# A six-sublayer decoder on one core: in the feed-forward, the down product moves behind the next tile's gate and up, the sigmoids move ahead of the rounding, and the layer norm's last step moves from the vector to the scalar engine

## The chip, the core and the metric

The kernel runs on one core of one Trainium2 chip. The metric is the device time of one execution in microseconds (us), of which the median over several runs is taken. The engines meant below are TensorE (PE in the profile; PEld is its weight loads), VectorE (DVE), ScalarE (ACT), GpSimd (POOL) and the sync engine's DMA queue (SP). Each engine works through its own instructions in the order in which they were written; semaphores (`G["..."]`) join them.

## The reference, cut to what matters

The model is two decoder layers of three sublayers each on x of 4 sequences of 256 tokens and 256 features; after each sublayer the sum is layer-normed. The change touches the third sublayer, a feed-forward in which weights are rounded to -1, 0, 1 and activations to 8 bits:

```python
def _quant_act(x):
    scale = jnp.maximum(jnp.max(jnp.abs(x), axis=-1, keepdims=True), EPS) / 127.0
    return clip(round(x / scale), -128, 127) * scale      # forward value
gate = jax.nn.sigmoid(bitlinear(x, w_gate))     # 256 -> 1024
up = bitlinear(x, w_up)                         # 256 -> 1024
out = bitlinear(gate * up, w_down)              # 1024 -> 256
x = _layernorm(x + out)       # (v - mean) / sqrt(var + eps)
```

The sublayer behind it is an attention over latent keys and values. Its weights are folded on the chip first (a product of `w_qT` with `w_kd` and of `w_vd` with `w_oh` for each pair of heads), and that folding is done inside the feed-forward's loop.

## The kernel before

The 1024 tokens are eight tiles of 128 rows (`NT` = 8, t = 0 to 7), two to a sequence. The feed-forward runs as a loop over t from 0 to 8 written out by hand on four engines; nothing but the written order and the semaphores sets the order of work. For tile t:

- `f_gate_up(t)` (PE, L1883): eight bf16 products of 512 columns into banks 1 to 4 (the gate and the up in two halves c). It needs the sigmoid of the tile before for the gate's banks and the product `hh` of the tile before for the up's banks.
- `f_gate(t)` (ACT, L862): two sigmoids of 128x512, `f_sig`.
- `f_hidden(t)` (DVE, L1287): two products `hh` = gate * up (L1292), the largest of each row (L1295), four tiny steps to the row's scale (`f_hsc`, L1299) and one more (L1300).
- rounding (ACT, L880): `hr` = `hh` times the scale plus a magic number, `f_hround`.
- `f_hidden_quant(t)` (DVE, L1303): the magic number off again, `hq` in bf16, `f_hq`.
- `f_hiddenT(t)` (PE, L1974): eight bf16 transposes into bank 5; ACT copies them to `hqT` (L876).
- `f_down(t)` (PE, L1985): eight products into bank 6, `f_y`.
- `f_out(t)` (DVE, L1308): adds the residual (L1311), then the row's mean and variance (L1050, L1051), `ln_var`.
- `rstd_of(16 + t)` (POOL, L520): variance plus epsilon (L524), power -0.5 (L527), `ln_rstd`.
- `ln_end(16 + t)` (DVE, L1053): the normed row into `x_row` (L1056), `ln_done`.

Two more tasks run in the same loop. `d_fold(t)` (PE, L1992) is the folding for pair t of heads: four f32 products of 64 columns and two of 256 into bank 7, each recorded as two matmuls, which ACT copies out (`d_folded`, L837, lines L839 and L842). `d_fold(0)` waits for the transfers of `w_oh`, `w_qT` and `w_qr` (issued at L456 to L460, when the sublayer before has ended), and each later one for the copies of the one before. POOL's `rotate` (L567) works on folded weights in the first six steps, each ahead of `rstd_of` of the same step; its first one waits for the same transfers. Also in the loop are transposes of the quantized input of later sequences (`f_transpose`, copied by ACT's `f_rowsT`) and of finished sequences (`to_xT`, copied by ACT's `xT_copy`), and, in step 1, the last two tiles' input quantization (`f_round` on ACT L761, `f_quant` on DVE L1171).

The order within step t of the loop is, before the change: on PE `f_hiddenT(t-1)`, `f_down(t-1)`, `f_gate_up(t+1)`, `d_fold(t-1)`, transposes. On ACT: copy of `hqT(t-1)`, rounding of t, `f_gate(t+1)`, (step 1: two `f_round`), `d_folded(t-1)`, copies of transposes. On DVE: `f_hidden(t)`, `f_out(t-1)`, `f_hidden_quant(t)`, (step 1: two `f_quant`), `ln_end(t-1)`. After the loop PE goes on with `d_fold(7)` and `d_latent(0)`, the first product of the next sublayer, which waits for `d_folded(7)`.

Of the kernel before, what the change touches and what calls it, by code (L numbers as in the profile page):

```python
# [35 lines left out]
ACT = mybir.ActivationFunctionType  # L36
ALU = mybir.AluOpType
# [6 lines left out]
NT = B * TPB  # L44
# [87 lines left out]
def build(nc, d, xs, ys, out):  # L132
    with ExitStack() as ctx:
        def sb(name, shape, dt=F32):
            return ctx.enter_context(nc.sbuf_tensor(name, shape, dt))
# [7 lines left out]
        def sem(name):  # L143
            return ctx.enter_context(nc.semaphore(name))
# [40 lines left out]
        mhalf = sb("mhalf", [P, 1])  # L185

        x_ids = sb("x_ids", [P, NT, E + 2])
        x_row = x_ids[:, :, 0:E]
        xT = sb("xT", [P, KT, B * S])
        res = sb("res", [P, 4, E])  # L190
        stats = sb("stats", [P, 4, 6])
        mv = sb("mv", [P, 4, 2])
        nmr = sb("nmr", [P, 4])
        rstd = sb("rstd", [P, 4])
# [168 lines left out]
        G = {n: sem(n) for n in names}  # L363
# [141 lines left out]
        def _(pool):  # L505
            g = nc.gpsimd
# [10 lines left out]
            pool.dma_start(cbias[:, :], d["cbias"]).then_inc(G["ld_cbias"], 16)  # L517
            steps = [0]

            def rstd_of(n):  # L520

                s = n % 4
                pool.wait_ge(G["ln_var"], n + 1)
                g.tensor_scalar(rstd[:, s:s + 1], mv[:, s, 1:2], LN_EPS, None, ALU.add).then_inc(G["pool_step"], 1)  # L524
                steps[0] += 1
                pool.wait_ge(G["pool_step"], steps[0])
                g.tensor_tensor(rstd[:, s:s + 1], rstd[:, s:s + 1], mhalf[:, :], ALU.pow).then_inc(G["ln_rstd"], 1)  # L527


            def a_mixed_values(b):  # L530
# [52 lines left out]
            for n in range(NT):  # L583
                if n < 2:
                    rotate(w_ki[:, :, LAT:P], w_kr[:, :, :], LAT, KV1, n)
                elif n < 2 + 2 * KT:
                    k, half = divmod(n - 2, 2)
                    rotate(w_qe[:, k, :, LAT:P], w_qr[:, k, :, :], P, H1, half)
                rstd_of(2 * NT + n)

            def norm_p(p):
                for h in (2 * p, 2 * p + 1):
# [52 lines left out]
            for t in range(NT):  # L645
                n = 5 * NT + t
# [7 lines left out]
        def _(act):  # L654
            a = nc.scalar
# [140 lines left out]
            for b in range(B):  # L796
# [7 lines left out]
                for c in range(CP):  # L804
                    n = CP * b + c
# [26 lines left out]
                if b > 0:  # L832
                    act.wait_ge(G["w_scale"], b)
                    a.activation(w_f32[:, b - 1, :], w_f32[:, b - 1, :], ACT.Identity, scale=wsi[:, b - 1:b],
                                 bias=magic[:, :]).then_inc(G["w_round"], 1)

            def d_folded(t):  # L837
                act.wait_ge(G["d_w"], t + 1)
                a.activation(w_qe[:, :, 2 * t:2 * t + 2, 0:LAT],  # L839
                             PS[7][:, 0:2 * KT * LAT].rearrange("p (k h c) -> p k h c", k=KT, h=2),  # L840
                             ACT.Copy).then_inc(G["d_w_sb"], 1)
                a.activation(w_vo[:, t, :], PS[7][:, 256:256 + E], ACT.Copy).then_inc(G["d_w_sb"], 1)  # L842
# [19 lines left out]
            def f_gate(t):  # L862
                if t in (0, NT - TPB):
                    act.wait_ge(G["f_fac"], 1 if t == 0 else 2)
                for c in range(2):
                    act.wait_ge(G["f_gu"], 4 * t + 2 * c + 1)
                    if 2 * t + c >= 2:
                        act.wait_ge(G["f_h"], 2 * t + c - 1)
                    a.activation(sg[:, c, :], PS[1 + 2 * c][:, :], ACT.Sigmoid,
                                 scale=fs[:, t, 3:4]).then_inc(G["f_sig"], 1)  # L870

            f_gate(0)
            for t in range(NT + 1):
                if t > 0:
                    act.wait_ge(G["f_hqT"], t)
                    a.activation(hqT[:, (t - 1) % 2, :, :], PS[5][:, :].bitcast(BF16).rearrange("p (k t) -> p k t", k=FF // P),  # L876
                                 ACT.Copy).then_inc(G["f_hqT_sb"], 1)
                if t < NT:
                    act.wait_ge(G["f_hsc"], t + 1)
                    a.activation(hr, hh[:, t % 2, :], ACT.Identity, scale=fh[:, t % 2, 3:4],  # L880
                                 bias=magic[:, :]).then_inc(G["f_hround"], 1)
                if t + 1 < NT:
                    f_gate(t + 1)
                if t == 1:
                    f_round(NT - 2)
                    f_round(NT - 1)
                if 0 < t < NT:
                    d_folded(t - 1)
                if t % TPB == 0 and t // TPB + 1 < B:
                    f_rowsT(t // TPB + 1)  # L890
                if t >= 3 and t % TPB:
                    xT_copy(1, t // TPB - 1)
# [30 lines left out]
            for p in range(NP + 4):  # L923
# [8 lines left out]
                if p < NP:  # L932
                    for h in (2 * p, 2 * p + 1):
                        for j, (at, z) in enumerate(((0, 1), (1, 3))):
                            if j == 0:
# [3 lines left out]
                                         bias=dmx[:, h % 8, j:j + 1],  # L939
# [82 lines left out]
            for t in range(NT):  # L1022
                n = 5 * NT + t
                act.wait_ge(G["ln_rstd"], 5 * NT + 2 * (t + 1))
                a.activation(x_row[:, t, :], res[:, n % 4, :], ACT.Identity, scale=rstd[:, n % 4:n % 4 + 1],
                             bias=nmr[:, n % 4:n % 4 + 1]).then_inc(G["ln_done"], 1)
# [3 lines left out]
        def _(dve):  # L1030
            v = nc.vector
            steps = [0]
# [7 lines left out]
            def link(ins):  # L1040

                ins.then_inc(G["dve_step"], 1)
                steps[0] += 1
                dve.wait_ge(G["dve_step"], steps[0])

            def ln_begin(n, add):

                s = n % 4
                link(add(res[:, s, :]))
                link(v.bn_stats(stats[:, s, :], res[:, s, :]))  # L1050
                v.bn_aggr(mv[:, s, :], stats[:, s, :]).then_inc(G["ln_var"], 1)  # L1051

            def ln_end(n):  # L1053
                s, t = n % 4, n % NT
                dve.wait_ge(G["ln_rstd"], n + 1)
                v.tensor_scalar(x_row[:, t, :], res[:, s, :], mv[:, s, 0:1], rstd[:, s:s + 1], ALU.subtract,  # L1056
                                ALU.mult).then_inc(G["ln_done"], 1)
# [160 lines left out]
            for b in range(B):  # L1218
# [15 lines left out]
                for c in range(CP):  # L1234
                    n = CP * b + c
# [72 lines left out]
            def f_out(t):  # L1308
                n = 2 * NT + t
                dve.wait_ge(G["f_y"], t + 1)  # L1310
                ln_begin(n, lambda o: v.scalar_tensor_tensor(out=o, in0=PS[6][:, 0:E], scalar=fh[:, t % 2, 4:5],  # L1311
                                                             in1=x_row[:, t, :], op0=ALU.mult, op1=ALU.add))

# [15 lines left out]
            for t in range(NT + 1):  # L1329
                if t < NT:  # L1330
                    f_hidden(t)
                if t == 0:

                    for n in (NT - 2, NT - 1):
                        ln_end(NT + n)
                    for n in (NT - 2, NT - 1):
                        f_scales(n)
                    f_factors(NT - TPB, NT)
                if t > 0:
                    f_out(t - 1)  # L1340
                if t < NT:
                    f_hidden_quant(t)
                else:
                    d_split_x(0)
                if t == 1:
                    f_quant(NT - 2)
                    f_quant(NT - 1)
                if t > 0:
                    ln_end(2 * NT + t - 1)


            def d_query(p):
# [239 lines left out]
        def _(pe):  # L1592
# [392 lines left out]
            def f_down(t):  # L1985
                pe.wait_ge(G["f_hqT_sb"], t + 1)
                pe.wait_ge(G["ln_var"], 2 * NT - 1 if t == 0 else 2 * NT + t)
                for k in range(FF // P):
                    ins = mm(PS[6][:, 0:E], hqT[:, t % 2, k, :], w_ff[:, 2, k * E:(k + 1) * E], start=k == 0, stop=k == FF // P - 1)
                ins.then_inc(G["f_y"], 1)  # L1990

            def d_fold(t):  # L1992

                if t == 0:
                    pe.wait_ge(G["ld_lat"], 96)
                    pe.wait_ge(G["ld_wq"], 32)
                    pe.wait_ge(G["ld_wo"], 16)
                    pe.wait_ge(G["ln_var"], 2 * NT)
                else:
                    pe.wait_ge(G["d_w_sb"], 2 * t)  # L2000
                g = 2 * t // (H1 // KV1)
                for k in range(KT):
                    for i in range(2):
                        at = (2 * k + i) * LAT
                        mm(PS[7][:, at:at + LAT], w_qT[:, 2 * t + i, k * P:(k + 1) * P], w_kd[:, g, :])
                for i in range(2):
                    ins = mm(PS[7][i * LAT:(i + 1) * LAT, 256:256 + E], w_vd[:, g, :], w_oh[:, 2 * t + i, :])
                ins.then_inc(G["d_w"], 1)
# [24 lines left out]
            for t in range(NT + 1):  # L2033
                if t > 0:
                    f_hiddenT(t - 1)
                    f_down(t - 1)
                if t + 1 < NT:
                    f_gate_up(t + 1)
                if 0 < t < NT:
                    d_fold(t - 1)  # L2040
                if t % TPB == 0 and t // TPB + 1 < B:
                    f_transpose(t // TPB + 1)
                if t >= 3 and t % TPB:
                    pe.wait_ge(G["f_qT_sb"], min(t // TPB + 2, B))
                    to_xT(1, t // TPB - 1)
# [309 lines left out]
```

## Time and profile before

| | us |
|---|---|
| median of 3 runs | 855.43 (853.38, 855.43, 862.85) |
| the profiled execution | 851.29 |
| its span | 849.4 |
| PE busy | 717.7 (84%) |
| DVE busy | 441.4 (52%) |
| ACT busy | 397.4 (47%) |
| POOL busy | 203.4 (24%) |

The span is the time from the first to the last instruction of the profiled execution; 1.9 us lie around it. Busy time is a sum over the whole span, so it says little of one stage: the feed-forward's loop runs from about 335 us to 399 us of the span. Matmuls' ends are modelled in the records, and a granted clock of 1.00 is TensorE's full speed, 0.50 half of it.

### The profile page before, as it was taken

Reading aid. Unit: us, or ns where it says so; the run is one execution under the profiler, and the core shown is the slowest. Engines: PE = TensorE matmul, PEld = TensorE weight load, DVE = VectorE, ACT = ScalarE, POOL = GpSimd, SP = SyncE. Lnnn points to the kernel's source line nnn. Section 1 sums busy time; section 2 is a strip of 40 time slices with the busy share of each in tenths; the row PEclk is TensorE's granted clock in tenths of the full one; section 3 lists DMA queues with packets and bytes.
Section 4 is the critical chain, followed back from the end, with each engine's and each line's share of the span. In section 5 each row is a group of like instructions: output and inputs, shape, how many; then the busy total and the mean of one; then the engine's idle time right before and its main releaser. Section 6 shows DMA issues by size and latency. Waiting matters only on the chain.

```text
span 849.4 us, 13794 instructions
## 1 busy us (share of the span) xinstructions
PE 717.7 (84%) x4888; PEld 577.3 (68%) x4893; DVE 441.4 (52%) x1040; ACT 397.4 (47%) x1091; POOL 203.4 (24%) x351
## 2 busy tenths in 40 slices
PE   6887889999999997587989999998776279999960
PEld 4665778989889885355878888887665236666640
DVE  2676764675865845785545454444247712222214
ACT  3987664475555643664656454554321022222212
POOL 2454300000100101362123232333103602222224
PEclk9998999999999999898989999999989579999995
DMA  8993002202203101401000000000290211111104
GB/s 316 368 317 74 2 1 78 78 1 79 78 1 117 39 1 62 186 1 54 22 1 1 1 2 1 1 2 1 88 431 20 75 38 44 44 50 43 43 31 148
DMA packets 32258, 62.48 MB, mean 74 GB/s; under 512 B 2724, under 2 KB 26984, under 8 KB 29896
## 3 DMA queue, kind: packets, MB, share of 16 engines
q1 hardware_dynamic: 30184, 56.48, 19.4%
q0 software_dynamic: 2016, 5.22, 1.8%
q8 instruction: 37, 0.61, 0.3%
q14 instruction: 21, 0.17, 0.1%
HBM read 46.24 MB, written 15.55 MB: 73 GB/s over the span
## 4 chain that ended last, share of the span: by engine, by line
PE 59%; DVE 14%; ACT 14%; POOL 5%; DMA 4%; issue 4%; SPq 0%; POOLq 0%; DVEq 0%; ACTq 0%
PE banks L1594 39%; PE bank L1594 20%; ACT arena L706 4%; DVE U_split L1119 3%; ACT arena L937 2%; ACT U_split L725 2%; POOL xs L620 2%; DMA arena<-in_w_qr 2%; POOL rstd L527 1%; DVE mx L1073 1%; POOL rstd L524 1%; DVE arena L1292 1%; DMA ys<-arena 1%; ACT arena L744 1%; DVE fh L1295 1%
## 5 line engine op out<-in xcount | busy, mean ns | idle before, releaser
L1594 PE MATMUL banks<-arena 128*128 (+4 forms) x816 | 189.4, 426 | 3.8 <-DVE arena L1067 2.3
L1594 PEld LDWEIGHTS banks<-arena 128*128 128x128 f32 (+2 forms) x816 | 111.1, 184 | 49.8 <-issue 38.0
L1594 PE MATMUL bank<-U_split 128*128 128x256 f32 (+1 forms) x864 | 115.9, 290 | 16.1 <-DVE U_split L1119 14.6
L1594 PEld LDWEIGHTS bank<-U_split 128*128 128x128 f32 x864 | 108.8, 194 | 20.4 <-issue 16.5
L1594 PE MATMUL banks<-U_split 128*128 128x256 f32 (+1 forms) x624 | 101.7, 313 | 1.4 <-DVE U_split L1192 1.4
L1594 PE MATMUL banks<-cst,arena 128*128 128x128 f32 (+1 forms) x594 | 84.2, 277 | 17.3 <-DMA arena<-xs 11.8
L1594 PEld LDWEIGHTS banks<-cst,arena 128*128 128x128 f32 (+1 forms) x594 | 69.9, 142 | 39.0 <-issue 25.3
L1594 PEld LDWEIGHTS banks<-U_split 128*128 128x128 f32 x624 | 86.2, 193 | 10.5 <-issue 5.0
L937 ACT ACTIVATE arena<-banks,dmx 128x128 f32<-128x128 f32 (+1 forms) x128 | 52.4, 418 | 76.0 <-DVE dmx L1393 76.0
L524 POOL TENSOR_SCALAR rstd<-mv 128x1 f32<-128x1 f32 x48 | 14.7, 307 | 304.4 <-DVE mv L1051 280.8
L595 POOL TENSOR_SCALAR arena<-arena,dri 128x128 f32<-128x128 f32 (+1 forms) x128 | 52.0, 425 | 140.8 <-DVE dri L1359 140.8
L1119 DVE TENSOR_TENSOR U_split<-arena,U_split 128x512 fp32r<-128x512 f32 (+5 forms) x76 | 57.4, 778 | 17.0 <-ACT U_split L725 16.3
L1594 PE MATMUL bank<-arena 128*32 128x64 f32 (+5 forms) x716 | 48.2, 279 | 15.9 <-DVE arena L1440 8.1
L706 ACT ACTIVATE arena<-arena,mx 128x128 f32<-128x128 f32 x128 | 49.5, 390 | 9.7 <-DVE mx L1073 9.7
L1594 PEld LDWEIGHTS bank<-arena 128*32 128x32 f32 (+3 forms) x716 | 31.4, 123 | 32.7 <-issue 11.1
L725 ACT ACTIVATE U_split<-arena 128x512 fp32r<-128x512 f32 (+5 forms) x76 | 50.1, 700 | 3.8 <-PE bank L1594 3.8
L1555 DVE COPY arena<-banks 128x512 f32<-128x512 f32 x23 | 15.9, 692 | 68.3 <-PE banks L1594 68.3
L725 ACT ACTIVATE U_split<-banks 128x512 fp32r<-128x512 f32 (+1 forms) x44 | 24.1, 578 | 48.9 <-PE banks L1594 48.9
L1594 PE MATMUL banks<-wk_hi,U_split 128*128 128x256 f32 (+1 forms) x208 | 42.6, 295 | 0.0
L993 ACT ACTIVATE arena<-banks 128x256 f32<-128x256 f32 x23 | 8.8, 384 | 71.2 <-PE banks L1594 71.2
L550 POOL TENSOR_TENSOR arena<-arena,rinv 128x1024 f32<-128x1024 f32 x16 | 30.4, 1900 | 45.8 <-DVE rinv L1077 45.8
L642 POOL DMA_INDIRECT ys<-arena x23 | 23.9, 1040 | 70.8 <-ACT arena L993 68.4
(213 smaller groups left out, 1198.7 us busy)
## 6 DMA issues: line engine op xcount, KB each, us to landing
arena<-in_w_exp SPq DMA_DIRECT2D x8, 1536.0 KB, 14.2
xs<-arena SPq DMA_DIRECT2D x8, 1032.0 KB, 14.2
arena<-in_ctxT SPq DMA_DIRECT2D x4, 1601.0 KB, 7.4
arena<-in_ctx SPq DMA_DIRECT2D x4, 1536.0 KB
arena<-in_w_f SPq DMA_DIRECT2D x3, 1024.0 KB, 12.6
arena<-xs SPq DMA_DIRECT2D x23, 129.0 KB, 2.1
w_x<-in_w_x SPq DMA_DIRECT2D x9, 256.0 KB, 8.2
arena<-in_w_oh SPq DMA_DIRECT2D x1, 2048.0 KB, 7.8
```

The lines of the kernel that those rows point to most:

```text
L524: g.tensor_scalar(rstd[:, s:s + 1], mv[:, s, 1:2], LN_EPS, None, ALU.add).then_inc(G["pool_step"], 1)
L550: g.tensor_tensor(sm[:, n % 4, :, :], sm[:, n % 4, :, :], rinv[:, n % 4, :].unsqueeze(2).broadcast_to([P, H0F, P]), ALU.mult).then_inc(G[" ...
L595: g.tensor_scalar(dp[:, h % 6, a:z, :], dp[:, h % 6, a:z, :], dri[:, h % 8, j:j + 1], 1.0, ALU.mult, ALU.mult).then_inc(G["d_norm"], 1)
L620: g.indirect_dma_start(xs_words, bass.IndirectOffsetOnAxis(ap=tok_rows[:, c, t:t + 1], axis=0), x_ids[:, t, 0:z], None).then_inc(G["r_scat ...
L642: g.indirect_dma_start(ys, bass.IndirectOffsetOnAxis(ap=y_ids[:, slot:slot + 1], axis=0), yt[:, slot, :], None).then_inc(G[f"m_st{slot}"], 16)
L706: a.activation(sm[:, n % 4, h, :], sm[:, n % 4, h, :], ACT.Exp, bias=mx[:, n % 4, h:h + 1], accum_out=rsum[:, n % 4, h:h + 1]).then_inc(G[ ...
L725: a.activation(r32(out), src, ACT.Copy, **k).then_inc(G[s], 1)
L937: a.activation(dp[:, h % 6, at:z, :], PS[2 + h % 2][:, at * P:z * P].rearrange("p (c k) -> p c k", k=P), ACT.Exp, bias=dmx[:, h % 8, j:j + 1],
L993: a.activation(yt[:, slot, :], PS[4][:, 0:E], ACT.Copy).then_inc(G["m_y_sb"], 1)
L1119: v.tensor_tensor(r32(out), src, r32(high).bitcast(F32), ALU.subtract).then_inc(G[s], 1)
L1555: v.tensor_copy(hT, PS[2][:, :].rearrange("p (m t) -> p m t", m=FM)).then_inc(G["m_hT_sb"], 1)
L1594: return nc.tensor.matmul(o, w, x, start=start, stop=stop, **k)
```

## The change

On PE the down product goes from ahead of the next tile's gate and up to behind it, and `d_fold` goes from behind the gate and up to ahead of it. On ACT the sigmoids of tile t+1 go ahead of the rounding of tile t. The normed row is no longer written by DVE but by ACT, as rstd * x - mean * rstd, for which POOL works out -mean * rstd in a third small instruction; ACT issues it in step t behind `d_folded(t-1)` and ahead of the copies of transposes. DVE has a wait more, from the fifth tile on, for a row buffer that ACT has read.

```diff
--- before.py
+++ after.py
@@ -517,14 +517,19 @@
             pool.dma_start(cbias[:, :], d["cbias"]).then_inc(G["ld_cbias"], 16)
             steps = [0]
 
-            def rstd_of(n):
+            def rstd_of(n, centre=False):
 
                 s = n % 4
                 pool.wait_ge(G["ln_var"], n + 1)
                 g.tensor_scalar(rstd[:, s:s + 1], mv[:, s, 1:2], LN_EPS, None, ALU.add).then_inc(G["pool_step"], 1)
                 steps[0] += 1
                 pool.wait_ge(G["pool_step"], steps[0])
-                g.tensor_tensor(rstd[:, s:s + 1], rstd[:, s:s + 1], mhalf[:, :], ALU.pow).then_inc(G["ln_rstd"], 1)
+                g.tensor_tensor(rstd[:, s:s + 1], rstd[:, s:s + 1], mhalf[:, :], ALU.pow).then_inc(G["pool_step" if centre else "ln_rstd"], 1)
+                if centre:
+
+                    steps[0] += 1
+                    pool.wait_ge(G["pool_step"], steps[0])
+                    g.tensor_scalar(nmr[:, s:s + 1], mv[:, s, 0:1], rstd[:, s:s + 1], -1.0, ALU.mult, ALU.mult).then_inc(G["ln_rstd"], 1)
 
 
             def a_mixed_values(b):
@@ -586,7 +591,7 @@
                 elif n < 2 + 2 * KT:
                     k, half = divmod(n - 2, 2)
                     rotate(w_qe[:, k, :, LAT:P], w_qr[:, k, :, :], P, H1, half)
-                rstd_of(2 * NT + n)
+                rstd_of(2 * NT + n, centre=True)
 
             def norm_p(p):
                 for h in (2 * p, 2 * p + 1):
@@ -869,23 +874,31 @@
                     a.activation(sg[:, c, :], PS[1 + 2 * c][:, :], ACT.Sigmoid,
                                  scale=fs[:, t, 3:4]).then_inc(G["f_sig"], 1)
 
+            def f_rows(t):
+                n = 2 * NT + t
+                act.wait_ge(G["ln_rstd"], n + 1)
+                a.activation(x_row[:, t, :], res[:, n % 4, :], ACT.Identity, scale=rstd[:, n % 4:n % 4 + 1],
+                             bias=nmr[:, n % 4:n % 4 + 1]).then_inc(G["ln_done"], 1)
+
             f_gate(0)
             for t in range(NT + 1):
                 if t > 0:
                     act.wait_ge(G["f_hqT"], t)
                     a.activation(hqT[:, (t - 1) % 2, :, :], PS[5][:, :].bitcast(BF16).rearrange("p (k t) -> p k t", k=FF // P),
                                  ACT.Copy).then_inc(G["f_hqT_sb"], 1)
+                if t + 1 < NT:
+                    f_gate(t + 1)
                 if t < NT:
                     act.wait_ge(G["f_hsc"], t + 1)
                     a.activation(hr, hh[:, t % 2, :], ACT.Identity, scale=fh[:, t % 2, 3:4],
                                  bias=magic[:, :]).then_inc(G["f_hround"], 1)
-                if t + 1 < NT:
-                    f_gate(t + 1)
                 if t == 1:
                     f_round(NT - 2)
                     f_round(NT - 1)
                 if 0 < t < NT:
                     d_folded(t - 1)
+                if t > 0:
+                    f_rows(t - 1)
                 if t % TPB == 0 and t // TPB + 1 < B:
                     f_rowsT(t // TPB + 1)
                 if t >= 3 and t % TPB:
@@ -1308,6 +1321,8 @@
             def f_out(t):
                 n = 2 * NT + t
                 dve.wait_ge(G["f_y"], t + 1)
+                if t >= 4:
+                    dve.wait_ge(G["ln_done"], n - 3)
                 ln_begin(n, lambda o: v.scalar_tensor_tensor(out=o, in0=PS[6][:, 0:E], scalar=fh[:, t % 2, 4:5],
                                                              in1=x_row[:, t, :], op0=ALU.mult, op1=ALU.add))
 
@@ -1345,8 +1360,6 @@
                 if t == 1:
                     f_quant(NT - 2)
                     f_quant(NT - 1)
-                if t > 0:
-                    ln_end(2 * NT + t - 1)
 
 
             def d_query(p):
@@ -2033,11 +2046,12 @@
             for t in range(NT + 1):
                 if t > 0:
                     f_hiddenT(t - 1)
-                    f_down(t - 1)
+                if 0 < t < NT:
+                    d_fold(t - 1)
                 if t + 1 < NT:
                     f_gate_up(t + 1)
-                if 0 < t < NT:
-                    d_fold(t - 1)
+                if t > 0:
+                    f_down(t - 1)
                 if t % TPB == 0 and t // TPB + 1 < B:
                     f_transpose(t // TPB + 1)
                 if t >= 3 and t % TPB:
```

## Rows read from the trace of the kernel before

**Rows 1.** Chain of waits, 335 to 361 us: start us, us, what.
```profile
335.87 14.26 DMA arena<-in_w_qr
...
353.08 1.28 DVE arena L1292 x2
...
360.28 1.28 DVE arena L1292 x2
```

**Rows 2.** Timeline of one period: start us, us, engine, line, work, [idle before, releaser].
```profile
353.56 1.05 PE L1594 MATMUL bank<-w_ff,arena 128*128 128x256 bf16 x8 [1.12 <-ACT arena L876]
...
354.66 1.67 PE L1594 MATMUL banks<-w_ff,arena 128*128 128x512 bf16 x7
...
356.17 1.00 PE L1594 MATMUL bank<-w_kd,arena 128*128 128x64 f32 x8
...
356.47 1.24 ACT L880 ACTIVATE arena<-arena,magic,fh 128x1024 f32<-128x1024 f32 x1 [2.97 <-DVE fh L1299]
...
357.10 0.65 PE L1594 MATMUL bank<-arena,w_vd 128*64 128x256 f32 x4
...
357.40 0.18 DVE L1051 BATCH_NORM_AGGREGATE mv<-stats 128x2 f32<-128x6 f32 x1
...
357.62 1.25 ACT L869 ACTIVATE arena<-banks,fs 128x512 f32<-128x512 f32 x2
...
357.74 0.69 DVE L1306 TENSOR_SCALAR arena<-arena 128x1024 bf16<-128x1024 f32 x1 [0.17 <-ACT arena L880]
...
358.49 0.62 PE L1594 MATMUL banks<-ident,arena 128*128 128x128 bf16 x8 [0.41 <-DVE arena L1306]
...
359.18 1.18 DVE L1056 TENSOR_SCALAR x_ids<-res,mv,rstd 128x256 f32<-128x256 f32 x1 [0.74 <-POOL rstd L527]
```

**Rows 3.** Timeline, DVE, where it waited for the down product.
```profile
346.64 0.48 DVE L1311 SCALAR_TENSOR_TENSOR res<-bank,fh,x_ids 128x256 f32<-128x256 f32 x1 [0.79 <-PE bank L1594]
...
347.72 0.66 DVE L1306 TENSOR_SCALAR arena<-arena 128x1024 bf16<-128x1024 f32 x1
```

**Rows 4.** Timeline around the landing of the transfers.
```profile
343.63 1.02 ACT L876 ACTIVATE arena<-banks 128x1024 bf16<-128x1024 bf16 x1 [1.15 <-PE banks L1594]
...
349.16 0.59 ACT L761 ACTIVATE arena<-x_ids,magic,fs 128x256 f32<-128x256 f32 x1
...
349.78 0.29 DVE L1171 TENSOR_SCALAR arena<-arena 128x256 bf16<-128x256 f32 x1 [1.40 <-ACT arena L761]
...
350.22 1.08 PE L1594 MATMUL bank<-w_kd,arena 128*128 128x64 f32 x8 [1.26 <-issue]
```

**Rows 5.** Windows: stretch us, length, PE busy, other engines where shown, PEclk, DMA share, GB/s.
```profile
341.00:341.50 0.50, 0.00 (x0) 0.50 0.99 426
...
350.00:353.00 3.00, 2.21 (x20) 1.62 (x20) 0.90 (x3) 1.67 (x4) 2.41 (x6) 1.00 0.00 0
...
360.30:364.00 3.70, 3.13 (x13) 1.67 (x14) 3.53 (x10) 0.84 (x2) 2.33 (x2) 0.65 0.00 0
```

**Rows 6.** Timeline, PE, the folding at half clock.
```profile
390.88 1.81 PE L1594 MATMUL bank<-w_kd,arena 128*128 128x64 f32 x8
```

**Rows 7.** Timeline, the loop's end and the next sublayer's first product.
```profile
393.00 0.69 DVE L1306 TENSOR_SCALAR arena<-arena 128x1024 bf16<-128x1024 f32 x1 [0.16 <-ACT arena L880]
...
397.85 0.48 DVE L1311 SCALAR_TENSOR_TENSOR res<-bank,fh,x_ids 128x256 f32<-128x256 f32 x1 [3.28 <-PE bank L1594]
...
399.10 0.22 POOL L524 TENSOR_SCALAR rstd<-mv 128x1 f32<-128x1 f32 x1 [4.98 <-DVE mv L1051]
...
399.28 0.38 ACT L839 ACTIVATE arena<-bank 128x256 f32<-128x256 f32 x1 [2.57 <-PE bank L1594]
...
400.08 1.05 PE L1594 MATMUL bank<-xT,w_kvc 128*64 128x256 f32 x4 [0.85 <-ACT arena L842]
```

**Rows 8.** Timeline, the last layer norm, where ACT already writes the row.
```profile
835.70 0.22 POOL L524 TENSOR_SCALAR rstd<-mv 128x1 f32<-128x1 f32 x1
...
836.96 0.60 ACT L1025 ACTIVATE x_ids<-res,nmr,rstd 128x256 f32<-128x256 f32 x1 [0.72 <-POOL nmr L649]
```

## Prediction

> **What bounds the kernel now.** The profiled execution took 851.29 us, 4.1 us under the median of the three runs (855.43). The sum below is of differences, made against that execution's trace; I add it to the median.
>
> I read the chain of waits first. In the feed-forward's loop [rows 1] it holds two things: a transfer that ends at 350.1, and then the vector engine, which comes back to the same instruction (the first product of gate and up, L1292) every 7.20 us, from 353.08 to 360.28. Then the timeline of that period [rows 2], to see why. DVE finishes the variance at 357.6, takes the magic number off until 358.43, and then waits for POOL's power before it writes the normed row, from 359.18 to 360.28. That row copy shows 1.18 us with POOL's rotation beside it. TensorE has no part in this chain. The down product, the next tile's gate and up, and the folding stand in one piece of 4.19 us (353.56 to 357.75; one of the eight gate and up matmuls has no record), and then it waits for `hq`. So DVE and its wait for POOL set the period, and everything on PE lies beside it.
>
> **Normed row to ACT.** It removes from DVE the wait of 0.75 us and the row's 1.1 us, 1.85 us of each period. Without them the DVE and ACT round would be 5.35 us: from 353.08 to the end of `hq` at 358.43 [rows 2]. On ACT it adds a copy of 0.60 us, which the last layer norm has already in this form [rows 8]. ACT's work for a tile is then 1.02 (copy of `hqT`, [rows 4]) + 1.25 + 1.24 [rows 2] + 0.80 (the two folding copies, up to PE's start behind them, [rows 7]) + 0.60, and in most periods one more copy about as long: 5.5 us. It fits in the period found below.
>
> **The order on PE.** This is what now decides. A period on PE is `hiddenT(t-1)`, the folding, gate and up of t+1, and only then `down(t-1)`. On DVE `f_out(t-1)` stands ahead of `f_hidden_quant(t)`, and PE's next period starts with the transposes of that `hq(t)`. This closes a ring that before had gaps in it: 0.06 us from `hq` to the transposes, 0.62 for them [rows 2], 4.19 for the same three pieces in the new order and 0.1 between them and the transposes, 0.04 to DVE, and from the start of `f_out` to the end of `hq` 1.74 us (346.64 to 348.38, [rows 3]). That is 6.75 us, with PE at full clock. Beside it, and hidden: the sigmoids (they can start 0.4 and 1.3 us into gate and up), and then the rounding, which ends some 5.5 to 6.0 us into the period where `hq` wants it at 6.0. The cover is thin: if ACT gets 0.5 us later, that adds to each period. The row copy is issued behind POOL's three steps and ahead of the copy of `hqT`, which delays that copy to 2 to 3.4 us into the period; `down` wants it at 3.8.
>
> **The head.** `d_fold(0)` waits for the three transfers, the last of which lands at 350.1 [rows 1]; nothing in the change issues them sooner. Before, `down(0)` and `gate_up(2)` had been done by then, and only the folding waited (350.22, [rows 4]). Now both stand behind the folding, and `hq(1)`, the two late quantizations and `hh(2)` stand behind them. PE idles from 343.6 to 350.2. The clock was at 0.50 in an idle stretch at 341.0, and full over 350 to 353, where PE had just run the down product and gate and up [rows 5]; so I take the first folding at half clock. At full clock it lasts 1.58 us (356.17 to 357.75, [rows 2]); at half clock its first part has 1.81 where that has 1.00 [rows 6], so about 2.9. Then: folding to 353.1, gate and up 1.7 to 354.8, down 1.05 to 355.9, `f_out` and `hq(1)` 1.74 to 357.7, quantizations 0.29 + 0.59 + 0.29 with their hand-overs [rows 4] to 359.0. The folding copies come on ACT behind the second rounding of 0.59 and let `d_fold(1)` start at 359.3; with 4.2 + 0.2 + 1.74, `hq(2)` ends at 365.5. Before it ended at 358.4: **+7.1 us**.
>
> TensorE: Matmul & The Clock Gate of the Trainium skill ("What's actually happening") says that the throttled clock is the default and that activity releases it. By that rule the folding at 350.2 is at 1.2 GHz and the head costs +7.1; by the nearest row, the same folding in this very place at 2.4 GHz, it would cost +5.8 and the total would be 1.3 us less.
>
> **The middle.** From `hq(2)` to the last `hq(7)` it took 393.69 - 358.43 = 35.26 us [rows 2, 7]. After: four periods of 6.75, and the last one, in which PE has no gate and up, at DVE's 5.35: 32.35. **-2.9 us**.
>
> **The end.** From the last `hq` to `f_out(7)` 4.16 us before [rows 7], with transposes of another sequence in between and PE at half clock. After, those transposes come earlier: 0.06 + 0.62 + 1.02 + 1.05 + 0.15 = 2.9 at full clock, 4.1 at half. I take **-0.6**. Then `d_latent(0)` needs the folding copies of ACT, which now stand behind the last normed row: `f_out` to POOL's start 1.25 [rows 7], POOL's start to the row copy 1.26 [rows 8], the copy 0.5 before the next can start, 0.80 for the folding copies and the hand-over [rows 7]: 3.8 us, where it was 2.23 (397.85 to 400.08). **+1.6 us**, on a path that goes on without slack into the next sublayer.
>
> POOL's third step is in the 1.26. DVE's added wait is for a copy that ended three tiles ago: nothing. Sum: 7.1 - 2.9 - 0.6 + 1.6 = **+5.2 us**, so 855.43 + 5.2 = **860.6 us**. Low end of the unknown terms: head at full clock and end at 2.9, +3.3. High end: end at half clock and ACT 0.5 us late in each of four periods, +7.8.
>
> **Rivals.**
> 1. *PE's half-clock phases count.* Before, a phase of mean clock 0.65 over 3.7 us [rows 5] cost nothing, since DVE led; it holds 2.6 us at half, so 1.3 us of lost work, and in the new ring that is time. Against it: PE will be busy 4.8 of 6.75 us. For it: the two long gaps behind the head. Three such phases make it 5.2 + 3.9 = +9.1, 864.5 us; from nearly three on the result is slower by over 1%.
> 2. *DVE leads after all.* If `down` were hidden behind DVE's other work, five periods of 5.35 would be 26.75 for 35.26: -8.5; with the cheaper head of +5.8, -0.6 and +1.6 that makes -1.7, 853.7 us. Against it stands the order on PE: `down` is the fourth piece, and DVE has only 3.4 us of work ahead of `f_out`.
> 3. *The transfers are no wait.* If they landed before the first transposes end, the head would cost nothing and the stall before (hq at 348.4, `hh(2)` at 353.08, 4.7 us) would go: with the ring's periods -4.7 - 2.9 - 0.6 + 1.6 = -6.6, with DVE's -12.2 (843.2). The landing at 350.1 speaks against it; 14.26 us of transfer do not shrink by a reorder of engines.
>
> **Chances.** One per cent, 8.6 us, is about what a measurement of this kernel can tell from no change. The forecast's own case (+2 to +8.5) has 0.62, rival 1 0.18, rival 2 (-5 to +2) 0.14, rival 3 in its fast form 0.06. So slower 0.18, within 1% 0.76, faster 0.06. The range takes in the unknown costs, most of rivals 1 and 2 and the spread of the runs: 852.5 to 867.5.
>
> **What would show it.** In the profile after: `d_fold(0)` first on PE behind the transposes of tile 0, at 350.2 and with the clock at 0.50, then `gate_up(2)` and `down(0)`; `hh(2)` near 359 where it was at 353.1; periods of 6.7 to 6.8 us with `f_out` (L1311's successor) waiting for PE each time; no row copy on DVE; `d_latent(0)` behind a row copy on ACT. The prediction is wrong if DVE's `f_out` shows no wait for PE, if the periods are near 5.4, or if `hh(2)` starts before 355.

## The result, and the profile after

The changed kernel takes 868.05 us (median of 5 runs, 862.37 to 870.26), the kernel before 856.15 (5 runs, 853.38 to 862.85): ratio 1.017, 95% interval 1.0125 to 1.0215. The ratio is worked out from the fast executions alone and is not the quotient of the two medians, which is 1.014. The kernel is slower, beyond the predicted range (852.5 to 867.5) and by more than twice the predicted 5.2 us. The two profiled executions differ by 11.1 us (862.37 and 851.29, spans 860.5 and 849.4); the one after is the fastest of its five.

I cut both traces at the same five instructions: the start of tile 1's first product of gate and up (DVE), the ends of `hq(2)` and `hq(7)`, the starts of `f_out(7)` and of `d_latent(0)` (PE), and the first exponential of the attention behind the loop (ACT, L937, L950 after).

| stretch | before | after | difference | predicted |
|---|---|---|---|---|
| head: `hh(1)` to the end of `hq(2)` | 16.0 | 23.5 | +7.5 | +7.1 |
| middle: to the end of `hq(7)` | 35.3 | 32.4 | -2.9 | -2.9 |
| `hq(7)` to `f_out(7)` | 4.2 | 4.4 | +0.2 | -0.6 |
| `f_out(7)` to `d_latent(0)` | 2.2 | 3.8 | +1.6 | +1.6 |
| `d_latent(0)` to the first exponential | 10.1 | 14.1 | +4.0 | 0 |
| from there to the end | 439.3 | 441.0 | +1.7 | 0 |

What stands ahead of `hh(1)` was 1.0 us shorter in the profile after. So the head, the middle and the tail came out as forecast, the stretch from `hq(7)` to `f_out(7)` missed by 0.8 us, and the large miss lies behind the loop.

The head, in the timeline of the changed kernel:

```profile
341.56 1.03 PE L1607 MATMUL banks<-ident,arena 128*128 128x128 bf16 x8 [3.92 <-DVE arena L1319]
...
349.02 1.94 PE L1607 MATMUL bank<-w_kd,arena 128*128 128x64 f32 x8 [6.43 <-issue]
...
351.95 2.63 PE L1607 MATMUL banks<-w_ff,arena 128*128 128x512 bf16 x7
...
354.42 1.04 PE L1607 MATMUL bank<-w_ff,arena 128*128 128x256 bf16 x8
...
355.50 0.48 DVE L1326 SCALAR_TENSOR_TENSOR res<-bank,fh,x_ids 128x256 f32<-128x256 f32 x1 [10.64 <-PE bank L1607]
...
358.37 1.28 DVE L1305 TENSOR_TENSOR arena<-arena,banks 128x512 f32<-128x512 f32 x2
```

This answers to [rows 4]. PE is idle for 6.4 us, then folds at half clock (1.94 us for the eight matmuls that had 1.08), then does gate and up, which still begins at half clock (2.5 us to the down product, where the forecast took 1.7), then the down product, and DVE has waited 10.64 us for it. `hh(2)` starts at 358.37 where it started at 353.08.

One period of the middle, the answer to [rows 2]:

```profile
385.20 0.62 PE L1607 MATMUL banks<-ident,arena 128*128 128x128 bf16 x8 [1.40 <-DVE arena L1319]
...
385.66 1.06 PE L1607 MATMUL bank<-w_kd,arena 128*128 128x64 f32 x8
...
386.26 0.60 ACT L880 ACTIVATE x_ids<-res,nmr,rstd 128x256 f32<-128x256 f32 x1 [1.81 <-POOL nmr L532]
...
387.23 1.90 PE L1607 MATMUL banks<-w_ff,arena 128*128 128x512 bf16 x8
387.25 1.01 ACT L887 ACTIVATE arena<-banks 128x1024 bf16<-128x1024 bf16 x1
...
388.96 1.04 PE L1607 MATMUL bank<-w_ff,arena 128*128 128x256 bf16 x8
...
389.32 1.23 ACT L893 ACTIVATE arena<-arena,magic,fh 128x1024 f32<-128x1024 f32 x1
390.04 0.48 DVE L1326 SCALAR_TENSOR_TENSOR res<-bank,fh,x_ids 128x256 f32<-128x256 f32 x1 [1.51 <-PE bank L1607]
...
391.12 0.66 DVE L1319 TENSOR_SCALAR arena<-arena 128x1024 bf16<-128x1024 f32 x1
```

Read it as a ring: transposes 385.20, folding, gate and up, down, `f_out` at 390.04, `hq` to 391.78, and the next transposes at 391.84. That is 6.64 us; with the transposes of other sequences before them the periods alternate with 6.80. The forecast was 6.75. The row copy left DVE, and in its place stands a wait for PE of 1.51 us.

The end, the answer to [rows 7]:

```profile
401.65 0.48 DVE L1326 SCALAR_TENSOR_TENSOR res<-bank,fh,x_ids 128x256 f32<-128x256 f32 x1 [4.37 <-PE bank L1607]
...
402.90 0.22 POOL L524 TENSOR_SCALAR rstd<-mv 128x1 f32<-128x1 f32 x1 [4.53 <-DVE mv L1064]
...
404.15 0.60 ACT L880 ACTIVATE x_ids<-res,nmr,rstd 128x256 f32<-128x256 f32 x1 [3.75 <-POOL nmr L532]
...
404.65 0.36 ACT L844 ACTIVATE arena<-bank 128x256 f32<-128x256 f32 x1
...
405.44 1.94 PE L1607 MATMUL bank<-xT,w_kvc 128*64 128x256 f32 x4 [1.17 <-ACT arena L847]
```

ACT holds the folding copies of pair 7 (L844) behind a row copy that waits for POOL: 3.8 us to `d_latent(0)`. And `d_latent(0)` itself takes 1.94 us where it took 1.05. The windows of PE say why. First the kernel before (stretch, length, PE busy, granted clock, DMA share, GB/s), then the changed one:

```profile
396.00:401.00 5.00, 3.39 (x24) 1.00 0.22 39
401.00:406.00 5.00, 4.37 (x30) 1.00 0.67 279
406.00:411.00 5.00, 5.00 (x34) 1.00 0.00 2
```

```profile
396.00:401.00 5.00, 1.17 (x13) 1.00 0.00 0
401.00:406.00 5.00, 3.83 (x19) 0.53 0.20 37
406.00:411.00 5.00, 4.37 (x15) 0.50 0.68 283
411.00:416.00 5.00, 5.00 (x22) 0.61 0.00 0
```

From 396 to 401 PE is now busy for 1.17 us, since the last down product waits for ACT, ACT for POOL. Behind that stretch the clock falls to 0.50, from 401.3 to 414.9. Before, a half-clock phase lay at 388.7 to 395.6, inside the loop. The chain of waits passes through PE there too, but only about 1.3 us of it counted: `hq(7)` ended on DVE at 393.69, and at full clock its transposes could have ended at about 394.4 instead of 395.64 (an estimate, with the 0.06 and 0.62 us of the other periods). Now the phase lies where PE leads for the whole stretch. The chain of waits before:

```profile
389.20 4.54 PE bank L1594 x20
393.74 1.91 PE banks L1594 x12
...
400.08 2.10 PE bank L1594 x12
...
402.79 1.13 PE bank L1594 x4
403.92 2.02 PE banks L1594 x16
...
410.15 1.73 ACT arena L937 x8
```

And after:

```profile
405.44 3.85 PE bank L1607 x12
...
409.90 2.07 PE bank L1607 x4
411.97 3.36 PE banks L1607 x16
...
419.55 1.73 ACT arena L950 x8
```

`d_latent(0)`, the first `d_keys`, and the transposes with the first query take 3.85, 2.07 and 3.36 us in this chain; before, they took 2.10, 1.13 and 2.02. The three differences add up to 4.03 us, the whole of what this stretch grew by.

### The profile page after: what moved, and what is told of

Read it like the earlier page. It is cut to its first block, busy times and chain, and to the rows that moved or that the text cites. A ratio compares the mean times of both kernels' runs of the same rounds, so it can differ in the third digit from the quotient of the medians.

```text
span 860.5 us, 13806 instructions
## 1 busy us (share of the span) xinstructions
PE 718.0 (83%) x4888; PEld 578.7 (67%) x4893; DVE 434.9 (51%) x1032; ACT 401.0 (47%) x1099; POOL 204.5 (24%) x359
## 4 chain that ended last, share of the span: by engine, by line
PE 38%; DVE 6%; ACT 5%; POOL 3%; DMA 2%; issue 1%; another core or an unknown queue 0%; SPq 0%; POOLq 0%; DVEq 0%
PE banks L1607 30%; PE bank L1607 8%; ACT arena L950 2%; POOL rstd L527 1%; POOL xs L625 1%; DMA ys<-arena 1%; ACT arena L957 1%; ACT U_split L730 1%; DVE U_split L1132 1%; DVE stats L1063 1%; POOL rstd L524 0%; DVE dmx L1406 0%; DVE arena L1367 0%; POOL arena L600 0%
## 5 line engine op out<-in xcount | busy, mean ns | idle before, releaser
L1607 PE MATMUL bank<-U_split 128*128 128x256 f32 (+1 forms) x864 | 117.8, 294 | 16.0 <-DVE U_split L1132 14.6
L1607 PEld LDWEIGHTS bank<-U_split 128*128 128x128 f32 x864 | 110.7, 198 | 20.3 <-issue 16.5
L1607 PE MATMUL banks<-cst,arena 128*128 128x128 f32 (+1 forms) x594 | 85.7, 280 | 21.2 <-DMA arena<-xs 13.9
L950 ACT ACTIVATE arena<-banks,dmx 128x128 f32<-128x128 f32 (+1 forms) x128 | 52.3, 417 | 74.2 <-DVE dmx L1406 74.2
L1607 PEld LDWEIGHTS bank<-arena 128*32 128x32 f32 (+3 forms) x716 | 31.5, 125 | 29.5 <-issue 15.7
## 6 DMA issues: line engine op xcount, KB each, us to landing
arena<-in_w_exp SPq DMA_DIRECT2D x8, 1536.0 KB, 14.1
```

Of the source, the lines that this page charges most:

```text
L950: a.activation(dp[:, h % 6, at:z, :], PS[2 + h % 2][:, at * P:z * P].rearrange("p (c k) -> p c k", k=P), ACT.Exp, bias=dmx[:, h % 8, j:j + 1],
L1607: return nc.tensor.matmul(o, w, x, start=start, stop=stop, **k)
```

## The experiments

All ratios are to the kernel before, run on the same chip, with their 95% intervals. The stretches are cut as in the table above.

**Folding last.** One part undone, the folding's place:

```diff
-                if 0 < t < NT:
-                    d_fold(t - 1)
                 if t + 1 < NT:
                     f_gate_up(t + 1)
                 if t > 0:
                     f_down(t - 1)
+                if 0 < t < NT:
+                    d_fold(t - 1)
```

> The changed kernel, but on PE the folding goes last in each step (behind the down product) instead of first; the down product stays behind gate and up. Theory (the folding's place is the cost: it closes the ring and puts the whole head behind the transfers): hq(2) ends within 1.5 us of the kernel before's distance from hh(1) (16.0 us) instead of 23.5, periods 6.0 to 6.6 us, then bound by POOL's three steps, the row copy and the copy of the transposed tile in ACT's queue; total 11 to 16 us under the changed kernel, ratio to before 0.995 to 1.003. Rival (the new place of the down product is the cost): periods stay near 6.7 and the ratio stays above 1.01.

Measured: 1.0016 (0.9982 to 1.0050), the profiled execution 10.1 us under that of the changed kernel. The head is 16.0 us, the periods alternate between 6.13 and 6.81, the longer above the expected band. Nearly the whole loss goes with this one move, the new place of the down product kept. The rival falls. Behind the loop a part stays: the clock is at 0.50 from 399.6 to 406.4, and `d_latent(0)` to the first exponential takes 12.9 us. What binds the periods now is the queue of ACT: the copy of `hqT`, which the down product needs, stands behind the row copy. A run below takes that away and gets 5.32.

**Row copy back on DVE**, both reorders kept (POOL's third step, `f_rows` and the added wait removed, `ln_end(2 * NT + t - 1)` back at the end of DVE's step):

> The changed kernel with the normed row written by DVE again (no third step on POOL); both reorders stay. Theory: the head stays at 23.5 us, the periods go from 6.7 to about 7.1 (+2 us in all), the end and tail lose the two waits of ACT's queue for POOL (-2.8 us), and the half-clock phase behind the loop (4 us) may go with them: 1 to 5 us under the changed kernel, ratio 1.008 to 1.015. Rival (the row copy in ACT's queue is the whole loss): ratio 1.00.

Measured: 1.0168 (1.0115 to 1.0221). Head 25.2 us, periods near 7.2, and the stretch behind the loop 13.9 us: the row copy is not the loss. The expected gain of 1 to 5 us didn't come, and the ratio lies above the expected band. The half-clock phase stayed (402.7 to 419.7), `hq(7)` to `f_out(7)` and the tail were only 0.2 and 0.3 us shorter (4.1 and 3.5), and the periods grew as foreseen. That the phase would go with ACT's wait was wrong.

**Rounding ahead of the sigmoids again**, on ACT:

> The changed kernel with the rounding ahead of the sigmoids on ACT again; the rest stays. Theory: the sigmoids and the rounding both have room in a ring of 6.7 us that PE and DVE set, so the periods stay at 6.6 to 6.9; the head ends up to 0.7 us sooner since the folding copies of pair 0 come sooner: ratio 1.011 to 1.019. Rival (the sigmoids ahead of rounding delay the rounding and with it hq): periods drop by 0.5 us or more, ratio under 1.010.

Measured: 1.0144 (1.0095 to 1.0193), periods 6.64 and 6.80 as in the changed kernel. This reorder does nothing in the ring, as expected. The head did not get shorter (25.3 us): PE is at half clock until 355, and again from 361.9 to 365.3, so that from `hq(1)` to `hq(2)` it is 9.3 us where the changed kernel's profile has 7.7.

**Only the first folding moved back:**

```diff
-                if 0 < t < NT:
+                if 1 < t < NT:
                     d_fold(t - 1)
...
                     f_down(t - 1)
+                if t == 1:
+                    d_fold(0)
```

> The changed kernel, with only the first folding, the one that waits for the transfers, moved behind gate_up(2) and down(0) in its step; all later foldings stay ahead of gate and up. Theory: this takes away the head's loss alone, hq(2) ends 16 to 17.5 us after hh(1) instead of 23.5, periods stay 6.7: 6 to 8 us under the changed kernel, ratio 1.000 to 1.010 (the lower end if the half-clock phase behind the loop does not fall). Rival (the head is caught up by something later, such as a later wait): ratio stays at 1.013 or more.

Measured: 1.0070 (1.0035 to 1.0105), head 20.5 us. Right in the ratio, only half right in the head. `hh(2)` starts 8.0 us after `hh(1)`. But `hq(2)` waits for `down(1)`, and ahead of that PE has the first folding, the transposes, the second folding and gate and up, at half clock from 350.1 to 360.3. The period that ends with `hq(2)` takes 13.66 us:

```profile
349.12 0.66 DVE L1319 TENSOR_SCALAR arena<-arena 128x1024 bf16<-128x1024 f32 x1
...
350.81 1.94 PE L1607 MATMUL bank<-w_kd,arena 128*128 128x64 f32 x8 [2.81 <-issue]
...
353.74 1.03 PE L1607 MATMUL banks<-ident,arena 128*128 128x128 bf16 x8
...
357.52 3.26 PE L1607 MATMUL banks<-w_ff,arena 128*128 128x512 bf16 x8
```

**Filler at the end.** To settle what the 4.0 us behind the loop are, products that compute nothing go where PE idles:

```diff
+            def filler(n):
+                for i in range(n):
+                    mm(PS[4][:, :], ident16[:, :], w_ff[:, 0, 0:512])
...
                     f_hiddenT(t - 1)
+                if t == NT:
+                    pe.wait_ge(G["f_h"], 2 * NT)
+                    filler(10)
...
             d_fold(NT - 1)
+            filler(5)
```

> The changed kernel with work that computes nothing: ten bf16 products of 512 columns on PE into a free bank after the transposes of tile 7, where PE idled from 398.0 to 400.4, and five more behind the last folding, ahead of d_latent(0). Each is about 0.21 us at full clock, so they fit the idle. Theory (the 4 us lost behind the loop, from d_latent(0) to the first exponential of the attention, 14.1 us for 10.1, are TensorE at half clock after the idle): the granted clock stays at 1.00 from 400 to 415, that stretch goes back to 10 to 10.6 us, and the kernel is 3 to 5 us under the changed one, ratio to before 1.007 to 1.014. Rival (the stretch is long for another reason, such as ACT's new order): the clock stays up and the stretch remains at 13 to 14 us.

Measured: 1.0092 (1.0064 to 1.0120). The windows of PE in this kernel:

```profile
396.00:401.00 5.00, 3.21 (x22) 1.00 0.00 0
401.00:406.00 5.00, 3.79 (x27) 1.00 0.36 103
406.00:411.00 5.00, 4.37 (x29) 1.00 0.52 216
411.00:416.00 5.00, 5.00 (x34) 1.00 0.00 0
```

The clock stays at 1.00, and `d_latent(0)` to the first exponential takes 10.07 us, as before, with the wait for the row copy (3.79 us) left as it was. So the 4.0 us are TensorE at half clock and nothing else. The rival falls. The profiled execution as a whole is 8.2 us under that of the changed kernel; its head is 1.0 longer, and 4.4 us of the gain lie behind the first exponential, which stays unexplained.

**The row copy alone**, in the kernel before:

> The kernel before with one part of the change alone: the normed row written by ACT, with POOL's third step. Theory: the head stays within 1.5 us of before (16.0 us), periods fall from 7.2 to 6.1 to 6.6 us (bound by POOL's steps, the row copy, the hqT copy, down), the tail grows by 1.6 us (f_out(7) to d_latent 3.8 us), and the half-clock phase may add up to 4: ratio 0.994 to 1.003. Rival (DVE and POOL were not the bound): periods stay at 7.2, ratio 1.001 to 1.008.

Measured: 1.0036 (1.0003 to 1.0069), just above the expected band and within the rival's, though the rival's own sign, periods of 7.2, is absent. The head is 15.7 us, the periods 6.84 (7.62 once), less gain than expected; the tail 3.8 us and the stretch behind it 14.7, with the clock at 0.50 from 395.6 to 412.7. What the shorter periods give, the end takes back.

**PE's order alone**, in the kernel before:

> The kernel before with the new order on PE alone (folding, gate and up, down); ACT and DVE as before. Theory: the head alone is lost, 7 to 9 us, periods stay at 6.9 to 7.3, the tail stays at 2.2 us; with the clock phase behind the loop up to 4 more: ratio 1.008 to 1.016. Rival (the order on PE is harmless and the moves on ACT make the loss): ratio under 1.004.

Measured: 1.0133 (1.0104 to 1.0162). Head 24.7 us, periods 7.2 (one of 8.8 at half clock), the tail 3.5 us where 2.2 was expected, the stretch behind it 14.2 us. PE's order alone makes a loss as large as the whole change, within the intervals.

**Rows a step later.** In the changed kernel, `f_rows(t - 2)` directly behind the copy of `hqT(t - 1)`, the last one behind `d_latent(0)` on ACT:

> The changed kernel with only the row copies moved a step later on ACT (the last behind the copies for d_latent); PE's order stays folding, gate and up, down. Theory (PE's ring through the folding and the down product sets the period, ACT has room in it): periods stay at 6.6 to 6.8, the head at 23.5 to 25; only the tail shortens, by 1.3 to 1.6 us, and the wait of the last down by 1: 1.5 to 3 us under the changed kernel, ratio 1.010 to 1.016. Rival (ACT's wait for POOL sets the period): periods of 6.2 or less, ratio under 1.009.

Measured: 1.0125 (1.0067 to 1.0184), periods 6.64 throughout. ACT's wait for POOL is not in the ring while the folding stands first. `f_out(7)` came 0.7 us sooner, but the tail was shorter by only 0.3 us, since the last folding ran at half clock. Behind it the kernel lost more than that: `d_latent(0)` to the first exponential took 16.7 us (14.1 in the changed kernel), with the clock at 0.50 from 401.0 to 421.5. The profiled execution is 1.3 us over the changed kernel's, so the expected gain of 1.5 to 3 us is not in it, though the ratio lies in the expected band.

**`hq` ahead of `f_out` on DVE**, in the changed kernel:

```diff
-                if t > 0:
-                    f_out(t - 1)
                 if t < NT:
                     f_hidden_quant(t)
-                else:
+                if t > 0:
+                    f_out(t - 1)
+                if t == NT:
                     d_split_x(0)
```

> The changed kernel with f_hidden_quant(t) ahead of f_out(t-1) on DVE, so that hq no longer waits for the down product. Theory (the ring runs through f_out): it is cut, and the next ring binds, transposes, folding, first half of gate and up, sigmoids, rounding, hq: 6.4 to 6.55 us, against 6.72; head shorter by 0 to 1.2 us: ratio 1.008 to 1.016. Rival (the ring is another): periods stay at 6.6 to 6.8 or grow.

A miss, and the rival's sign: 1.0213 (1.0156 to 1.0270), with periods of 8.7, 7.5, 8.9 and 7.5 us. In the two longer ones PE is at half clock for part of the time (371.2 to 374.6 and 384.7 to 391.6). The timeline of one at full clock:

```profile
375.26 0.69 DVE L1319 TENSOR_SCALAR arena<-arena 128x1024 bf16<-128x1024 f32 x1 [3.26 <-ACT arena L893]
...
376.84 0.18 DVE L1064 BATCH_NORM_AGGREGATE mv<-stats 128x2 f32<-128x6 f32 x1
...
378.46 0.60 ACT L880 ACTIVATE x_ids<-res,nmr,rstd 128x256 f32<-128x256 f32 x1 [2.68 <-POOL nmr L532]
...
379.44 1.01 ACT L887 ACTIVATE arena<-banks 128x1024 bf16<-128x1024 bf16 x1
...
380.35 1.26 ACT L874 ACTIVATE arena<-banks,fs 128x512 f32<-128x512 f32 x2
...
381.49 1.25 ACT L893 ACTIVATE arena<-arena,magic,fh 128x1024 f32<-128x1024 f32 x1
...
382.77 0.69 DVE L1319 TENSOR_SCALAR arena<-arena 128x1024 bf16<-128x1024 f32 x1 [2.04 <-ACT arena L893]
```

The ring through the down product is cut, but the variance now ends 1.8 us after `hq` starts instead of before it, POOL starts later, and ACT's queue comes due one behind the other: row copy, transposed tile, sigmoids, rounding, `hq`. That ring (375.26 to 382.77) was hidden before, with the thin cover that the prediction named. I had priced the next ring without what the edit itself moves on POOL.

**Folding last and rows later**, both at once:

> The changed kernel with the folding last on PE in each step, and each row copy on ACT a step later, behind the copy of hqT (the last one behind ACT's copies for d_latent), so that no copy that PE needs waits for POOL. Theory: head 15 to 17 us, periods 5.4 to 5.9 us (DVE's 5.35, ACT's 5.5 of work), the tail back at 2.2 to 2.5 us; 7 us less than before if the clock holds, 3 less if it falls behind the loop: ratio 0.990 to 0.998. Rival (with POOL out of the way the down product still closes a ring): periods stay at 6.1 or more, ratio 0.997 to 1.003.

Measured: 0.9949 (0.9911 to 0.9987). The head is 17.3 us, just above the expected 15 to 17. The periods are 5.32 us behind a first one of 5.45, DVE's own work, with no wait of note:

```profile
L1320 DVE TENSOR_SCALAR arena<-arena 128x1024 bf16<-128x1024 f32 x5 | 3.4, 687 | 0.5 <-ACT arena L895 0.3
L1327 DVE SCALAR_TENSOR_TENSOR res<-bank,fh,x_ids 128x256 f32<-128x256 f32 x5 | 2.4, 483 | 0.4 <-PE bank L1608 0.3
```

(DVE's groups from 360 to 387 us: busy us, mean ns, idle before.) In the changed kernel the second of these groups waits 8.2 us in six tiles (359 to 397 us):

```profile
L1326 DVE SCALAR_TENSOR_TENSOR res<-bank,fh,x_ids 128x256 f32<-128x256 f32 x6 | 2.9, 484 | 8.2 <-PE bank L1607 8.2
```

The middle is 26.7 us, 8.6 less than before, but the clock fell to half from 383.1 to 403.6, and the end took part of it back: 5.4 + 3.5 + 13.8 us where it was 4.2 + 2.2 + 10.1.

**Filler on that kernel** (five products behind the transposes of tile 6, five behind those of tile 7, three behind the last folding):

> The kernel of the run with the folding last and the row copies a step later, with filler products on PE that compute nothing: five behind the transposes of tile 6, five behind those of tile 7, three behind the last folding. There the half-clock phase lasted from 383 to 403 and the two stretches behind the loop took 3.5 and 13.8 us. Theory: the clock stays up at the end, those stretches go to 2.3 and 10.1, and the kernel is 4 to 6 us under that run: ratio to before 0.986 to 0.992. Rival (a filler of a few products doesn't hold the clock, or its half-clock phase starts earlier and elsewhere): ratio 0.993 to 0.998.

Measured: 841.33 us, 0.9858 (0.9804 to 0.9912), just below the expected band. The clock stays at 1.00 from 356 to 425; the three last stretches are 2.9 + 2.2 + 10.4.

**Each folding one step later still** (on PE as shown; ACT's `d_folded` moves a step later with it):

```diff
+                if t >= NT - 1:
+                    d_fold(t - 2)
                 if t + 1 < NT:
                     f_gate_up(t + 1)
                 if t > 0:
                     f_down(t - 1)
-                if 0 < t < NT:
-                    d_fold(t - 1)
+                if 1 < t < NT - 1:
+                    d_fold(t - 2)
```

> The kernel with the folding last and the row copies a step later, with each folding one step later still: the first now at the end of step 2, and in steps 7 and 8 ahead of the down product, where PE waits for the copy of hqT. Theory (the transfers still hold back everything behind the first folding, so hq(2) ended 17.3 us after hh(1)): the head falls to 11 to 14 us, periods stay at 5.3 to 5.5, and PE's busier end lowers the clock less or not at all: ratio 0.980 to 0.990. Rival (POOL's rotation, which waits for the same transfers, holds the head through the row copy on ACT): head stays at 16 to 17, ratio 0.992 to 0.997.

Measured: 842.67 us, 0.9879 (0.9821 to 0.9938). The head is 14.4 us, just over the expected 11 to 14, the middle 27.0, the end 3.2 + 2.3 + 11.9 with a short half-clock phase (392.3 to 395.7). This kernel and the one with filler on the better order both beat the one before and the changed one; they differ by less than their intervals.

## Why the prediction was wrong

*Its mechanism in the loop and three of its four terms were right.* The ring on PE (6.75 forecast, 6.64 and 6.80 measured), the head behind the transfers (+7.1 and +7.5) and the tail behind the row copy (+1.6 and +1.6) are in the trace of the changed kernel. The run with the folding last and the one with PE's order alone show that the folding's place makes the loss, not the row copy and not the sigmoids. For the first folding the prediction took the price at half clock, and PE did run it so (1.94 us for its first part, 1.08 before); at the full clock of its nearest row the head would have been forecast at +5.8, and it was +7.5. TensorE: Matmul & The Clock Gate of the Trainium skill ("What's actually happening") has the throttled clock as the default, which activity releases. This trace agrees: PE, idle since 342.6, was at 0.50 at 349.0 and back at 1.00 at 353.4, while it worked. Behind the loop it worked for far longer before the clock came back, from 401.3 to 414.9.

*The end* was forecast at -0.6 and was +0.2. PE was at full clock there; the cost is ACT's, which copies row 6 (398.41, behind POOL) and one more tile before it copies `hqT(7)` at 399.39. The forecast priced that queue for `d_latent(0)` and forgot it for the down product just ahead.

*The step that failed* is the last sentence of the end: the tail's delay lies "on a path that goes on without slack into the next sublayer", and that path was carried over at its old length. It is 4.0 us longer, where the sum had nothing, as PE, which leads there, ran 9.5 us of it at half clock. The filler shows that this is the whole of it. Rival 1 had the cause, half-clock phases that begin to count, but looked for them in the ring, at 1.3 us each, with 0.18. In the ring of the profiled execution there were none. The run with the rounding ahead of the sigmoids, whose later periods are the same, has one from 361.9 to 365.3, and its head is 1.6 us longer between `hq(1)` and `hq(2)`, about the rival's price. The idle stretch that counted was at the loop's end (1.17 us of work in five), and the price was set by what ran behind it.

*The rest.* In the profiles the kernel is 5.9 us worse than forecast: 0.4 in the head, 0.8 in the end, 4.0 at half clock behind the loop, 1.7 behind the first exponential, less 1.0 ahead of `hh(1)`. The 1.7 us stay open. From the first exponential to the end it is 435 to 441 us in all these kernels, without order, and the lower clock in the routing stage (0.68 after and 0.76 before, in the 70 us that start 230 us behind the first exponential) does not explain it: the run with filler at the end has 0.71 there and 436.5 us.

The timed medians differ by 11.9 us and the ratio of 1.017 is above the profiles' 1.013, though the interval holds both. The mean granted clock of each execution says where to look. The profiled one of the changed kernel has 0.926; the four others, at 867.8 to 870.3 us, have 0.916 to 0.920. The kernel before shows the same, in 23 executions on one chip: 844.8 us at 0.944, 860.3 us at 0.924. Which half-clock phases the four slower executions had in addition no trace here shows.

## What to carry to other kernels

Ask of each reordered in-order queue which ring it closes: here two engines were taken off the bound, and the new order tied PE's side task, the folding, to every tile. Work that waits for a transfer belongs behind all that doesn't need it, and a side task in the slot where its engine waits anyway. When the end of a stage makes PE wait longer, price the stage behind it at half clock too; a few idle-filling products are a cheap test of that price.

## What the runs showed of the hardware

Half-clock phases lasted much longer than the idle stretch ahead of them, though PE was busy again: 13.6 us behind 2.5 us of idle in the changed kernel, with 3.83, 4.37 and 5.00 us of work in each five, and 20 us behind 1.1 us of idle in the kernel with the folding last and rows later. Fifteen products of 512 columns, 3.4 us of work that computes nothing, kept the clock up and took 4.0 us off the stretch behind the loop. POOL's three steps for one row, from the end of the variance to the start of ACT's copy, take 1.3 us alone (402.81 to 404.15) and 1.7 us when DVE takes the magic number off beside the first of them (384.56 to 386.26); that the one causes the other no run tested. The time of a whole execution goes with its mean granted clock: the kernel before took 844.8 us at 0.944 and 860.3 us at 0.924.
